# Cross attention 0: the score banks are preset with the negated maxima by ScalarE and VectorE, in place of TensorE passes that add them

## What is computed

```python
x = x + _L0_xattn_ref(_layernorm(x), ctx_1024, ctx_1024, mask, Wq, bq, Wk, bk, Wv, bv, Wo, bo)
# inside: q = x Wq + bq ; k = ctx Wk + bk ; v = ctx Wv + bv, split into 16 heads of 64
# softmax(q k^T / 8, masked) v, heads joined, times Wo, plus bo
...
```

## Time and profile before

| | |
|---|---|
| median of three runs | 5865.0 us |
| profiled execution, span | 5863.6 us |
| first exponential of this cross attention | 410.3 us |
| last exponential | 2503.1 us |
| TensorE busy over the span | 5274.1 us, 90% |
| VectorE, ScalarE, GpSimd busy | 47%, 54%, 38% |

### The profile page before, as it was taken

One profiled execution on the slowest core, in us unless ns is written; L12 is line 12 of the kernel. 1 busy time (PEld: TensorE's weight loads), 2 busy tenths in 40 slices (PEclk: granted clock), 3 DMA queues, 4 the chain that ended last, 5 costly groups with the idle time before them and its releaser, 6 DMA issues. The chain is left out here.

```text
span 5863.6 us, 69367 instructions
## 1 busy us (share of the span) xinstructions
PE 5274.1 (90%) x28014; PEld 1717.5 (29%) x28014; DVE 2726.8 (47%) x3143; ACT 3176.0 (54%) x3203; POOL 2218.6 (38%) x1113
## 2 busy tenths in 40 slices
PE   8879999999999999989999689999886788888889
PEld 3213333333333333332243311111342111111123
DVE  5664545454545552015541400000246998898713
ACT  4455555555555555521122399999124677777761
POOL 1119898989888899915533000000000000000000
PEclk8869999999999999989999799999896799999999
DMA  1000000000000000010000120000203000000010
GB/s 50 15 1 1 1 1 1 1 1 1 1 1 1 1 1 1 1 41 1 2 1 4 52 84 11 20 11 2 80 25 123 13 11 11 11 11 11 7 46 31
DMA packets 64433, 100.77 MB, mean 17 GB/s; under 512 B 9846, under 2 KB 49880, under 8 KB 62000
## 3 DMA queue, kind: packets, MB, share of 16 engines
q1 hardware_dynamic: 63906, 95.50, 4.9%
q10 hardware_dynamic: 206, 0.83, 0.0%
HBM read 70.85 MB, written 25.31 MB: 16 GB/s over the span
## 5 line engine op out<-in xcount | busy, mean ns | idle before, releaser
L2433 ACT ACTIVATE Pr<-ps,key_bias 128x1024 f32<-128x1024 f32 x816 | 893.2, 1114 | 1015.4 <-PE ps L2325 1015.4
L2521 DVE TENSOR_REDUCE red<-ps 128x2 f32<-128x1024 f32 (+1 forms) x767 | 908.1, 1185 | 959.2 <-PE ps L2310 954.0
L2579 POOL TENSOR_TENSOR Ps<-Ps,Pr 128x1024 f32<-128x1024 f32 x400 | 944.3, 2361 | 215.9 <-ACT Pr L2433 215.9
L2588 POOL TENSOR_TENSOR Ps<-Ps,Pr 128x1024 f32<-128x1024 f32 x400 | 947.5, 2369 | 0.0
L3206 DVE TENSOR_REDUCE red<-ps 128x1 f32<-128x512 f32 (+3 forms) x1024 | 877.7, 908 | 94.0 <-PE ps L3079 74.7
L3162 ACT ACTIVATE Pr<-ps 128x1024 f32<-128x1024 f32 x816 | 786.2, 1021 | 228.5 <-PE ps L3089 227.9
L2323 PE MATMUL ps<-Q,Kr 64*128 64x512 f32 x3264 | 842.3, 594 | 0.5 <-DVE red L2521 0.2
L2342 PE MATMUL ps<-Pr,Vc 128*64 128x512 f32 x3264 | 790.1, 605 | 0.0
L3336 ACT ACTIVATE Pr<-ps 128x2048 f32<-128x2048 f32 x467 | 726.2, 2024 | 1.6 <-PE ps L3299 1.6
L3079 PE MATMUL ps<-Kp,Q 52*128 52x512 bf16 (+1 forms) x1664 | 441.8, 411 | 172.1 <-DVE red L3206 125.7
L544 POOL IOTA number<- 128x8 f32 x1 | 0.1, 139 | 1157.5 <-POOLq L89 1157.5
(11 more groups left out here) (580 smaller groups left out, 5197.2 us busy)
## 6 DMA issues: line engine op xcount, KB each, us to landing
L_dram_K<-parts SPq DMA_DIRECT2D x26, 384.0 KB, 3.1
Kp<-L_dram_K SPq DMA_DIRECT2D x14, 624.0 KB
L_dram_K<-parts SPq DMA_DIRECT2D x26, 256.0 KB, 2.9
wB<-L_ffn_shares SPq DMA_DIRECT2D x1, 6144.0 KB
w<-L_ffn_experts_w_dram SPq DMA_DIRECT2D x24, 256.0 KB
Kp<-L_dram_K SPq DMA_DIRECT2D x14, 416.0 KB
wB<-L_ffn_shares SPq DMA_DIRECT2D x1, 3584.0 KB, 12.4
ctx<-ctx_dram SPq DMA_DIRECT2D x13, 256.0 KB, 7.4
```

What stands on the lines that cost most here:

```text
L2433: nc.scalar.activation(Pr[:, t % 4, half].rearrange("p a n -> p (a n)"), ps[:, 2 * half:2 * half + 2, :].rearrange("p a n -> p (a n)"), AC ...
L2521: nc.vector.tensor_reduce(red[:, g // C % 2, q, :, g % C], ps[:, maxima_bank(g, s, steps, q):maxima_bank(g, s, steps, q) + 2, 0:ctx.keys_i ...
L2579: nc.gpsimd.tensor_tensor(into, into, src, ALU.add).then_inc(*summed0.up())
L2588: nc.gpsimd.tensor_tensor(into, into, src, ALU.add).then_inc(*summed1.up())
```

## The change

The passes with `ones` and `Qa` are gone. In their place the negated maxima are kept as full tiles (`seeds`: 128 equal rows, bf16), and one copy of 128x1024 from `seeds` into the two banks of a half is made before the scores of that half, which then accumulate on to it (`start=False`). `dve_seeds` and `act_seeds` share out the copies: VectorE has all those of half 1, and those of half 0 that follow a tile with a maximum in bank 0 (`behind`); ScalarE has the other ones of half 0, and issues them behind its exponentials of the tile before. That makes 529 copies on VectorE and 287 on ScalarE. A copy waits for the exponential that reads the bank, and for `rows_set` at a pair's first tile. `rows` is split into two steps with 128 columns each, `mz` becomes a tile of 2048 columns that VectorE fills with one broadcast copy, the values' projection moves behind the last maximum, the addition to `X` moves ahead of it, and the last chunk's maxima cover 512 columns where they go to banks 0 to 3. Some constants of the program's start that nothing reads are gone.

```diff
+    def behind(g, s, steps):
+        return [q for q in list(maxima_at(g, s, steps))[1:] if g >= LAG and maxima_bank(g, s, steps, q) == 0]
+    tile_turns = {KT * (j // C) + TPC * (j % C) + s: (g, s, steps) for g, j, steps in turns() for s in range(steps) if 0 <= j < N}
+    dve_seeds = [(t, half) for t in range(P * KT) for half in range(2) if half == 1 or t == 0 or behind(*tile_turns[t - 1])]
+    act_seeds = [(t, 0) for t in range(P * KT) if (t, 0) not in dve_seeds]
+    def seed(engine, copy, t, half, signal):
+        p = t // KT
+        if t:
+            engine.wait_ge(*exp_done.at(2 * (t - 1) + half + 1))
+        if t % KT == 0:
+            engine.wait_ge(*rows_set.at(2 * p + 2))
+        copy(ps[:, 2 * half:2 * half + 2, :], seeds[:, p % 2, half]).then_inc(*signal.up())
...
         def scores(j, s, half):
...
-            take_banks(2 * half, exp_done.at(2 * t + half + 1))
+            nc.tensor.wait_ge(*seeded(t, half))
+            taken[2 * half] = [exp_done.at(2 * t + half + 1)]
...
-                nc.tensor.matmul(ps[:, 2 * half + a, :], lhsT=Kr[head(a), j % 16, s * 128:(s + 1) * 128], rhs=Q[head(a), p % 3, sl], start=True, stop=False)
-            for a in range(2):
-                mm = nc.tensor.matmul(ps[:, 2 * half + a, :], lhsT=ones[head(a), :], rhs=Qa[head(a), p % 2, sl], start=False, stop=True)
+                mm = nc.tensor.matmul(ps[:, 2 * half + a, :], lhsT=Kr[head(a), j % 16, s * 128:(s + 1) * 128], rhs=Q[head(a), p % 3, sl], start=False, stop=True, skip_group_check=True)
...
-        def rows(p):
-            take_banks(4, rows_set.at(p + 1))
+        def rows(p, half):
+            take_banks(4, rows_set.at(2 * p + half + 1))
...
+                t = KT * (j // C) + TPC * (j % C) + s
+                if 0 <= j < N and (t + 1, 0) in act_seeds:
+                    seed(nc.scalar, nc.scalar.copy, t + 1, 0, seeded_by_act)
...
-                nc.vector.tensor_reduce(mz[:, :, :, 0], red[:, p % 2], AX, ALU.max, negate=True).then_inc(*rows_step.up())
-                nc.vector.wait_ge(*rows_step.at(3 * p + 2))
-                nc.vector.tensor_tensor(mz[:, :, :, 1], neg[:], mz[:, :, :, 0], ALU.subtract).then_inc(*rows_step.up())
+                nc.vector.wait_ge(*rows_step.at(2 * p + 1))
+                nc.vector.tensor_copy(mz[:].rearrange("p q a n -> p (q a) n"), neg[:].rearrange("p q a -> p (q a)").unsqueeze(2).to_broadcast([128, 16, 128])).then_inc(*rows_step.up())
```

More of the change, by code:

```diff
@@ L2244, in cross_0 @@
     Q, Qb = k.tile(stack, "Q", [128, 3, S]), k.tile(stack, "Qb", [128, 2, S], BF16)
-    Qa, ones = k.tile(stack, "Qa", [128, 2, S], BF16), k.tile(stack, "ones", [128, 128], BF16)
+    seeds = k.tile(stack, "seeds", [128, 2, 2, 2, HALF], BF16)
     by_act = (0, 2, 4, 5, 7)
@@ L2277, in others_at @@
         return [(item, p) for item, p in ((item, pair_for(g, s, turn, step)) for item, turn, step in
-                (("queries", -1, 1), ("rows", C, 1), ("sums", LAG + C, 1), ("output", LAG + C + 2, 2))) if p is not None]
+                (("queries", -1, 1), ("first_rows", C, 1), ("second_rows", C, 2), ("sums", LAG + C, 1), ("output", LAG + C + 2, 2))) if p is not None]
     def maxima_bank(g, s, steps, q):
@@ L2361, in queries @@
             mm.then_inc(*query_mm.up())
-        def rows(p):
-            take_banks(4, rows_set.at(p + 1))
[L2365 to L2368, removed]
+        def rows(p, half):
+            take_banks(4, rows_set.at(2 * p + half + 1))
+            nc.tensor.wait_ge(*rows_step.at(2 * p + 2))
+            for a in range(2):
+                for q in range(4):
+                    mm = nc.tensor.matmul(ps[:, 4 + a, q * 128:(q + 1) * 128], lhsT=mz[:, 4 * half + q, a, :], rhs=k.consts.ident16[:], start=True, stop=True)
             mm.then_inc(*rows_mm.up())
@@ L2385, in output @@
             mm.then_inc(*out_mm.up())
-        nc.tensor.wait_ge(*zeroed.at(2))
+        nc.tensor.wait_ge(*zeroed.at(1))
         for t in range(P):
@@ L2398, in pe @@
                 others = others_at(g, s)
-                last = [q for q in items[1:] if g >= LAG and maxima_bank(g, s, steps, q) == 0]
+                last = behind(g, s, steps)
                 between = [q for q in items[1:] if q not in last]
@@ L2410, in pe @@
                 if s == 0:
-                    keys_and_values(g + 1, j + 1)
+                    keys(g + 1, j + 1)
                 elif not others and g >= LAG:
@@ L2415, in pe @@
                 for item, p in others:
-                    {"queries": queries, "rows": rows, "sums": sums, "output": output}[item](p)
+                    if item in ("first_rows", "second_rows"):
+                        rows(p, ("first_rows", "second_rows").index(item))
+                    else:
+                        {"queries": queries, "sums": sums, "output": output}[item](p)
                 for q in last:
                     maxima(g, s, steps, q)
+                if s == 0:
+                    values(j + 1)
                 if 0 <= j and 0 < t <= KT * P and (j < N or s == 0):
@@ L2469, in act @@
                     nc.scalar.copy(Ur[:], ps[:, 6:8, :].rearrange("p a n -> p (a n)")).then_inc(*acc_copied.up())
[L2470 to L2475, removed]
+                for half in range(2):
+                    p = pair_for(g, s, C, 1 + half)
+                    if p is not None:
+                        nc.scalar.wait_ge(*rows_mm.at(2 * p + half + 1))
+                        if p >= 2:
+                            nc.scalar.wait_ge(*scored.at(2 * KT * (p - 1)))
+                        nc.scalar.copy(seeds[:, p % 2, half], ps[:, 4:6, :]).then_inc(*rows_set.up())
                 p = pair_for(g, s, LAG + C, 1)
```

83 lines of the change are left out of this document (48 added, 35 removed).

## The result

The changed kernel takes 5879.3 us, the kernel before 5860.1 (medians of nine runs each): a ratio of 1.0034, with a 95% interval of 1.0025 to 1.0044. It is slower by a third of a per cent, where 5834 us was forecast.

A forecast was written before the change was run, and what follows sets the result against it. TensorE was taken to bound the 90 turns with maxima beside scores, GpSimd the last pair. 5863.6 - 152 + 27 + 93 + 3 = 5834.6, stated as 5834 us; range 5755 to 5885, with 5800 to 5862 at 50%.

The forecast's parts named there:

- The last pair: Last pair, without maxima: bound by GpSimd, so shorter TensorE work gives nothing; it stays as before.
- the moved values: Values' projection, placed behind the last maximum by the change: the prediction's sum has no term for it.
- the prediction's own signs of being wrong: Ordinary turns not a microsecond shorter, special turns growing much less or more than 1 to 5 us, or GpSimd's additions lengthening.
- Removal, -152: TensorE, 354 tiles of the 90 turns: two passes of 0.215 us a tile go, saving 152 us.
- The ring through ScalarE, +27: Ordinary chunks: scores, two exponentials, preset copy, next scores take 4.27 against 4.12 us; 59 turns lose 0.45 each, 27 us.
- Boundaries, +93: Pair ends, `rows` turns, reciprocals, `output` and `queries`: VectorE's queue delays TensorE, 16, 23, 31, 17 and 7 us.
- the first turns, +3: First turns with rows and presets (g = 13): in sequence with nothing beside them, 3 us more.
- Rival 1: Boundary delays mostly hidden: no ring loss and half of the 93 us, giving 5761 us; 5730 to 5800 at 22%.
- about 23: Three-step turn with `rows`: forecast to grow from 17.97 to about 23 us in the profile after.
- takes nothing: Float32 scores directly following each other in tiles without `ones`: no cost taken; 0.11 us a joint would add 78 us.
- Rival 4: Float32 joints or longer VectorE queue cost more: no change to 5890 us; 23% together with a dearer ScalarE copy.
- rival 3: VectorE's preset copies hold up GpSimd's additions, making GpSimd the bound: 290 us more, 6150 us; 4%.

The follow-up runs named there:

- experiment 1: Kernel before, with the pass with `ones` left out and nothing in its place, so scores are not shifted: 5720.6 us, 0.9751.
- experiment 11: Changed kernel, ScalarE's presets cut to one bank of two; the other head's scores of that half stay unshifted: 5840.3 us, 0.9963.
- experiment 12: Changed kernel, VectorE's presets cut to one bank of two, ScalarE's whole; the other head's scores of these halves stay unshifted: 5846.3 us, 0.9972.
- experiment 4: Changed kernel, with the reciprocals between a tile's two reductions, ahead of the presets instead of behind them: 5865.9 us, 1.0006.
- experiment 10: Changed kernel; ScalarE presets half 1 where VectorE has half 0, reciprocals and `Ur` multiplication between reductions, ScalarE fills `mz` in halves: 5832.0 us, 0.9959.
- experiment 2: Kernel before, with only the values' projection moved behind the last maximum of the first tile: 5880.2 us, 1.0024.
- experiment 7: Changed kernel, with the values' projection put back behind the keys and ahead of the last maxima: 5952.0 us, 1.0148.
- experiment 3: Changed kernel, with `mz` filled by a VectorE reduction over one element instead of the copy: 5879.9 us, 1.0028.
- experiment 9: Changed kernel; ScalarE presets half 1 where VectorE has half 0, and ScalarE's presets move ahead of its once-a-pair copies: 5867.9 us, 1.0011.
- experiment 5: Changed kernel, presets exchanged: VectorE half 0 between reductions, ScalarE half 1 behind its exponentials and ahead of once-a-pair copies: 5956.3 us, 1.0159.

## Why the prediction was wrong

Two steps failed. The last pair was put at nothing, "bound by GpSimd", and lost 20.7 us, since presets behind held VectorE instructions left GpSimd without work; and the moved values were put at nothing and cost 16.7 us. None of the prediction's own signs of being wrong came: ordinary turns shortened by 1.01 us, the special ones grew by 2.0 to 5.5 us over their lengths without the pass (experiment 1), the additions did not lengthen. What failed was "the last pair as before".

The sum went by -152, +27, +93, +3, with nothing for the moved values and nothing for the last pair. Against the traces (89 turns, then what is behind them):

- **Removal, -152**: 138.9 in the turns (experiment 1). 98 of it in the 57 ordinary turns, just as worked out. The step counted the full 0.43 us a tile in the special turns too, where TensorE already waited in part. 13 us too much.
- **The ring through ScalarE, +27**: 28.9 (57 turns, 1097.5 us, against 1068.6 in experiment 11). Right in mechanism and size. The forecast's 59 turns were 57.
- **Boundaries, +93, and the first turns, +3**: from experiment 1 to the changed kernel these turns grow by 99.6 us, some 6 of which are the moved values. The sum was right, in part by luck; the parts less so. Turn 0 with the turn before it grew by 6.6 us a pair over experiment 1 (2.6 + 3.8 + 1.0 = 7.4 was said), turns 1 and 2 by 4.9 (5.1), turn 3 by 4.8 on average (2.8). What turn 3 costs more makes up for what the others cost less. Rival 1 is out: the delays do add up in full. Experiment 12 gives 41 of the 99.6 us back with shorter copies on VectorE, and experiment 4 takes 18.5 with another place in its queue, so the walk was right that VectorE's queue is behind much of it. Turn 3 fell only in the run that also moved the multiplication of `Ur` and the last reciprocals (to 24.6 in experiment 10, which changes other things too). The "about 23" for the three-step turn does not follow from the walk's own terms: 17.97 less three times 0.43 plus 3.8 is 20.5, and 21.3 was measured.
- **Moved values, 0**: the step that "takes nothing" for joints looked at the scores, and there it held. The cost was at the last maxima, which now stand between keys and values: 16.7 us (experiment 2). The order of the two programs shows the move; it was not priced. Rival 4 named dearer joints, in another place, and the time fell into its span, from no change to 5890.
- **The last pair, 0**: this is the step that failed most. "That pair is bound by GpSimd, and shorter TensorE work gives nothing there" is right, but a pair that GpSimd bounds loses whatever makes GpSimd wait, and it lost 20.7 us. What does it was on the page: `mz` is filled while the additions run, and a small VectorE instruction there had taken 1.31 us. So was the multiplication of `Ur` that took 2.91 beside an addition; rival 3 read that row for what VectorE does to GpSimd, and what came was the other way round. The text counted 1.2 us for the first wait, as a price of each pair's end, and not what a longer one would do where GpSimd is the bound and where, with the change, the scores wait for VectorE.

13 + 2 + 17 + 21 = 53 us, less 2 us that were set too high at the boundaries, are the 51 between the forecast of -29 and the +22 of the trace's turns and last pair. (The medians differ by 19.)

Of the last pair's 20.7 us, 9 to 10 are the held fill: experiments 7 and 3, in which VectorE's fill was not held, are shorter there by that much. Of the 10.7 that experiment 3 still has over the kernel before, 9.76 are GpSimd's one wait behind the held multiplication of `Ur`. That second half is read from the waits in the timeline and from experiment 10, and no run here changed it alone. A small part of both may be TensorE's clock. In the window 2270 to 2280 the granted clock was 0.66, right behind TensorE's wait of 6.70 us, and in 2340 to 2350, with the wait of 7.72 us, it was 0.56, where the kernel before has 1.00 in both windows. Both values lie between the two levels, 1.2 and 2.4 GHz (0.5 and 1.00), so some matmuls there ran at the lower one.
```profile
2270.00:2280.00 10.00, 7.24 (x28) 2.64 (x28) 3.93 (x3) 3.47 (x4) 2.83 (x2) 0.66 0.00 0
```
(Length, busy us of PE, PEld, DVE, ACT, POOL, then the granted clock.)

What stays open: why these two VectorE instructions are held in the last pair and hardly at the earlier ones. Nor has a run here given ordinary turns whole presets without the ring: the one attempt moved it to VectorE.

## What to carry to other kernels

When work goes from the bounding engine to two others, count it once in the regular stretch and once more wherever those engines have work of their own; here the first gave 57 us and the second took 59, which moving work about on the two engines brought down by 43 (experiment 10). In a loop through three engines, place each new copy by what is queued behind it: the same presets gave 5868, 5879 or 5956 us by their engine and place alone (experiments 9 and 5). And look at a stretch that the change should leave alone: its bound may depend on the engine that you just loaded.

## What the runs showed of the hardware

VectorE's cast of 2048 fp32 columns to bf16 in SBUF was held here for as long as GpSimd's additions followed each other without a gap: it took 11.00 us, and ended 1.1 us behind the last of them. The multiplication of `Ur`, with both operands in SBUF, did the same: 8.38 us, and its end is 1.1 us behind the last addition's. At an earlier pair's end the cast took 1.23, beside additions that were back to back too, but it was issued within 0.1 us of the end of one, and the next addition was the one held:
```profile
1182.52 2.36 POOL L2624 TENSOR_TENSOR Ps<-Ps,Pr 128x1024 f32<-128x1024 f32 x1
1184.77 1.23 DVE L2609 CAST mz<-neg 128x2048 bf16<-128x2048 f32 x1
1184.84 3.36 POOL L2633 TENSOR_TENSOR Ps<-Ps,Pr 128x1024 f32<-128x1024 f32 x1
```
(The changed kernel's timeline.) But the moment alone does not decide. In the changed kernel the fill that took 11.00 us was issued 0.66 us before the next addition began; in experiment 12 the fills of six pairs were issued 0.71 or 0.72 us before it, and took about 1.85 us each:
```profile
1166.77 1.85 DVE L2610 CAST mz<-neg 128x2048 bf16<-128x2048 f32 x1
1167.48 3.34 POOL L2634 TENSOR_TENSOR Ps<-Ps,Pr 128x1024 f32<-128x1024 f32 x1
```
What decides stays open. In experiment 1 an operation on only 16 columns took 15.54 us at that place:
```profile
2113.99 15.54 DVE L2562 TENSOR_TENSOR mz<-neg,mz 128x16 bf16<-128x16 f32 x1
```
The Trainium skill (SBUF — State Buffer, "Who interferes with whom") says that whichever of the two issues first gets the shared ports for that whole instruction, and that the other blocks. The trace agrees for one pair of instructions (3.36 us). By that rule the fill at 2260.56 would have begun with the end of one addition, at 2261.22; it came after four more. The same values written by a reduction took 2.29 us beside the same additions.

A copy from bf16 in SBUF to 1024 float32 columns of the accumulator took 1.02 us on ScalarE and 1.22 on VectorE, 0.60 and 0.69 for 512; GpSimd's additions were not longer for any of them (2.37 to 2.38 us on average).
